# A fused decoder layer on one core: orders of their own for the first and last three turns, and the head weights turned in the double bank

## The reference

```python
x = layernorm(x + attn(x, W_attn, W_proj))           # 16 heads of 8, causal
x = layernorm(x + xattn(x, ctx, ctx, WQ, WK, WV, WO, bO))   # 16 heads of 64, softmax
x = layernorm(x + ffn(x, router_w, router_b, expert_w))     # 16 experts, top 6
```

## Time and profile before

| what | value |
|---|---|
| median of 3 runs | 1102.06 us (1099.71 to 1102.68) |
| the profiled execution | 1102.16 us |
| its span | 1100.3 us |
| mean granted TensorE clock | 0.985 of full |
| instructions | 44821 |
| busy share: DVE, ACT, POOL | 90%, 68%, 36% |
| DMA moved | 25.15 MB, mean 23 GB/s |

### The profile page before, as it was taken

One profiled execution on the slowest core, in us unless ns is written; L12 is line 12 of the kernel. 1 busy time (PEld: TensorE's weight loads), 2 busy tenths in 40 slices (PEclk: granted clock), 3 DMA queues, 4 the chain that ended last, 5 costly groups with the idle time before them and its releaser, 6 DMA issues.

```text
span 1100.3 us, 44821 instructions
## 1 busy us (share of the span) xinstructions
PE 1026.7 (93%) x16344; PEld 873.7 (79%) x16344; DVE 987.3 (90%) x3179; ACT 752.7 (68%) x1608; POOL 398.4 (36%) x682
## 2 busy tenths in 40 slices
PE   4789999999999999999999999999999999999874
PEld 3678888888888888888888888888888888888763
DVE  5579999999999999999999999999999999999776
ACT  4577876667787666777666678766677876667541
POOL 3232343433344333334433333434333443333331
PEclk8899999999999999999999999999999999999997
DMA  6000000000000000000000000000000000000000
GB/s 159 21 21 22 27 26 25 19 10 19 24 24 24 24 19 5 24 24 24 24 19 13 16 24 24 24 24 19 10 19 24 24 24 24 19 5 16 7 7 10
DMA packets 29577, 25.15 MB, mean 23 GB/s; under 512 B 2528, under 2 KB 24544, under 8 KB 29536
## 3 DMA queue, kind: packets, MB, share of 16 engines
q1 hardware_dynamic: 29536, 24.57, 7.7%
HBM read 20.37 MB, written 4.19 MB: 22 GB/s over the span
## 4 chain that ended last, share of the span: by engine, by line
PE 69%; DVE 14%; issue 6%; POOL 5%; ACT 4%; ACTq 0%; DMA 0%; DVEq 0%; POOLq 0%; SPq 0%
PE ps_B L349 54%; PE ps_S L349 10%; DVE sums L769 8%; PE ps_B L476 5%; POOL rstd L905 2%; DVE stats L692 2%; DVE ps_B L769 2%; ACT x L647 1%; ACT yT L545 1%; DVE p L748 1%; PE ps_B L435 1%; POOL shift L907 1%; POOL rstd L902 1%; DVE mv L698 1%; POOL minus_mean L903 1%
## 5 line engine op out<-in xcount | busy, mean ns | idle before, releaser
L769 DVE SCALAR_TENSOR_TENSOR sums<-ps_B,gate,sums 128x128 f32<-128x128 f32 x896 | 242.7, 345 | 9.9 <-PE ps_B L349 4.7
L902 POOL TENSOR_TENSOR rstd<-mv,ln_eps_tile 128x2 f32<-128x2 f32 x96 | 18.9, 197 | 522.9 <-DVE mv L698 522.9
L912 POOL TENSOR_TENSOR p<-p,rowinv 128x1024 f32<-128x1024 f32 x64 | 122.0, 1907 | 129.2 <-DVE rowinv L725 129.2
L545 ACT ACTIVATE q2T<-ps_B 128x512 f32<-128x512 f32 x128 | 73.2, 601 | 133.0 <-PE ps_B L349 133.0
L349 PE MATMUL ps_B<-wo_sb,oT 128*128 128x128 f32 x1024 | 122.8, 278 | 0.0
L647 ACT ACTIVATE x<-ps_B,shift,rstd 128x128 f32<-128x128 f32 x192 | 77.5, 456 | 63.1 <-POOL shift L907 62.7
L349 PE MATMUL ps_B<-ex_hi,x2T_hi 128*128 128x512 f32 x256 | 114.7, 448 | 5.5 <-POOL x2T_lo L886 4.3
L349 PEld LDWEIGHTS ps_B<-wo_sb,oT 128*128 128x128 f32 x1024 | 116.7, 192 | 2.2
L349 PE MATMUL ps_B<-ex_lo,x2T_hi 128*128 128x512 f32 x256 | 101.9, 398 | 0.0
L349 PE MATMUL ps_B<-ex_hi,x2T_lo 128*128 128x512 f32 x256 | 101.7, 397 | 0.0
L736 DVE SCALAR_TENSOR_TENSOR allowed<-ps_B,const 128x512 f32<-128x512 f32 x128 | 87.6, 684 | 9.2 <-ACT relu L567 8.9
(11 more groups left out here) (120 smaller groups left out, 2930.8 us busy)
## 6 DMA issues: line engine op xcount, KB each, us to landing
xT<-in_x_t SPq DMA_DIRECT2D x32, 256.0 KB, 2.7
...
```

The lines of the kernel that those rows point to most:

```text
L545: return nc.scalar.activation(dst, src, ACT.Copy, scale=scale)
L769: done = V.scalar_tensor_tensor(after, ps[BANK[f"FF{4 * r + q}"]][:, C * e:C * e + C], gate[:, r, 4 * q + e:4 * q + e + 1], before, ALU.mu ...
L912: G.tensor_tensor(weights, weights, rowinv[:, r].unsqueeze(2).broadcast_to([P, H, T]), ALU.mult).then_inc(p2_ready, 1)
```

## The change

Turns -2, -1 and 0 and turns 30, 31 and 32 get lists of their own for each engine, in which every step carries its turn (`K@-1`, `FF0@NT`), so a step of a later turn can stand before steps of an earlier one. Turns 1 to 29 keep the old lists. The counting of bank fills is adapted. The six heads jobs become three (one for queries, keys and values each, eight transposes) in the bank S, early in turns -2 and -1, each waiting for its own load; the copies and differences of them become 1024 wide. `experts_hi` goes from GpSimd to ScalarE, and the expert weights are loaded into the room of oT, so the first `AC0` copy waits for `experts_lo`. The first loads are put in another order, and VectorE splits W_attn before it makes the masks. A part of the diff:

```diff
+FIRST = {
+    "SP": """
+        x_columns@-2 x_rows@-1 context@-1 x_columns@-1 x_columns@0 x_rows@0 context@0
+    """,
+    "PE": """
+        Q@-2 K@-2 heads0@-2 V@-2 S1_0@-2 S1_1@-2 S1_2@-2 S1_3@-2 heads1@-2 K@-1 Q@-1 Y@-1 V@-1 heads2@-2 PR@-1 S1_0@-1
+        S1_1@-1 K2_3@-1 K2_0@-1 K2_2@-1 X1T@-1 S1_2@-1 S1_3@-1 Q2_3@-1 Q2_1@-1 Q2_0@-1 K2_1@-1 V2_3@0 K@0 Q2_2@-1 Y@0 S2_0@0
+        Q@0 PR@0 V@0 V2_0@0 V2_1@0 V2_2@0 S2_1@0 X1T@0 K2_0@0 Q2_3@0 PT0b@0 PT0a@0 S1_0@0 S1_1@0 K2_2@0 K2_3@0 AC0@0 K2_1@0
+        S1_2@0 PT1b@0 PT1a@0 S1_3@0 AC1@0 WO0@0 WO1@0 Q2_1@0 Q2_0@0 Q2_2@0 X2T@0 LG@0
+    """,
+    "ACT": """
+        K@-2 queries_hi@-2 heads_hi0@-2 relu0@-2 relu1@-2 square0@-2 square1@-2 V@-2 relu2@-2 relu3@-2 square2@-2
+        heads_hi1@-2 square3@-2 K@-1 experts_hi@-2 queries_hi@-1 Y@-1 V@-1 heads_hi2@-2 relu0@-1 relu1@-1 square0@-1 K2_0@-1
+        norm1@-1 K2_3@-1 K2_2@-1 square1@-1 x1_hi@-1 relu2@-1 relu3@-1 square2@-1 square3@-1 Q2_3@-1 Q2_1@-1 Q2_0@-1 K2_1@-1
...
+    "DVE": """
+        keys_lo0@-2 keys_lo1@-2 queries_lo@-2 heads_lo0@-2 allow0@-2 allow1@-2 pieces0@-2 pieces1@-2 p1_0@-2 allow2@-2
+        p1_1@-2 allow3@-2 pieces2@-2 pieces3@-2 p1_2@-2 p1_3@-2 keys_lo0@-1 heads_lo1@-2 keys_lo1@-1 queries_lo@-1
+        projected@-1 stats1@-1 var1@-1 allow0@-1 heads_lo2@-2 pieces0@-1 allow1@-1 p1_0@-1 pieces1@-1 x1_lo@-1 p1_1@-1
+        allow2@-1 allow3@-1 pieces2@-1 pieces3@-1 p1_2@-1 p1_3@-1 row_max0@0 projected@0 less_max0@0 stats1@0 var1@0
+        keys_lo0@0 keys_lo1@0 row_sum0@0 row_inv0@0 queries_lo@0 x1_lo@0 row_max1@0 less_max1@0 row_sum1@0 row_inv1@0
...
+    "POOL": """
+        next_x_hi@-2 context_hi@-1 next_x_lo@-2 context_lo@-1 root1@-1 experts_lo@-2 next_x_hi@-1 bias_x1@-1 next_x_lo@-1
+        root1@0 context_hi@0 context_lo@0 shares0@0 shares1@0 next_x_hi@0 root2@0 next_x_lo@0 x2_hi@0 bias_x1@0 x2_lo@0
+    """,
+}
+LAST = {
...
+    "PE": """
+        S2_0@NT-2 Y@NT-2 PR@NT-2 V2_3@NT-2 V2_0@NT-2 S2_1@NT-2 V2_1@NT-2 V2_2@NT-2 X1T@NT-2 FF0@NT-2 PT0a@NT-2 PT0b@NT-2
+        Q2_3@NT-2 K2_0@NT-2 K2_3@NT-2 K2_2@NT-2 K2_1@NT-2 AC0@NT-2 FF4@NT-2 PT1a@NT-2 PT1b@NT-2 FF5@NT-2 FF1@NT-2 AC1@NT-2
+        WO0@NT-2 WO1@NT-2 FF2@NT-2 FF6@NT-2 Q2_1@NT-2 FF7@NT-2 FF3@NT-2 X2T@NT-2 Q2_0@NT-2 Q2_2@NT-2 LG@NT-2 S2_0@NT-1
+        S2_1@NT-1 FF0@NT-1 V2_3@NT-1 V2_0@NT-1 V2_1@NT-1 PT0b@NT-1 V2_2@NT-1 FF4@NT-1 PT0a@NT-1 AC0@NT-1 FF5@NT-1 PT1a@NT-1
+        PT1b@NT-1 FF1@NT-1 AC1@NT-1 WO0@NT-1 WO1@NT-1 FF2@NT-1 FF6@NT-1 FF7@NT-1 FF3@NT-1 X2T@NT-1 LG@NT-1 FF0@NT FF4@NT
+        FF5@NT FF1@NT FF2@NT FF6@NT FF7@NT FF3@NT
+    """,
+    "ACT": """
...
+        norm2@NT-2 X2T@NT-2 Q2_0@NT-2 Q2_2@NT-2 logit_exp@NT-2 norm3@NT-2 exp0@NT-1 V2_3@NT-1 V2_0@NT-1 V2_1@NT-1 exp1@NT-1
+        PT0b@NT-1 V2_2@NT-1 PT0a@NT-1 base3@NT-1 AC0@NT-1 PT1a@NT-1 PT1b@NT-1 AC1@NT-1 norm2@NT-1 X2T@NT-1 logit_exp@NT-1
+        norm3@NT-1 base3@NT norm3@NT
+    """,
+    "DVE": """
...
+        gate1@NT-2 var3@NT-2 row_max0@NT-1 less_max0@NT-1 gate2@NT-1 gate3@NT-1 gate4@NT-1 gate5@NT-1 gate6@NT-1
+        row_sum0@NT-1 gate7@NT-1 row_inv0@NT-1 row_max1@NT-1 gate8@NT-1 less_max1@NT-1 gate9@NT-1 gate10@NT-1 gate11@NT-1
+        gate12@NT-1 row_sum1@NT-1 gate13@NT-1 row_inv1@NT-1 gate14@NT-1 gate15@NT-1 weigh0@NT-1 weigh1@NT-1 attended@NT-1
+        stats2@NT-1 var2@NT-1 weigh2@NT-1 weigh3@NT-1 logits@NT-1 gate0@NT-1 gate1@NT-1 stats3@NT-1 var3@NT-1 gate2@NT
...
+    "POOL": """
+        root1@NT-2 shares0@NT-2 context_hi@NT-2 context_lo@NT-2 shares1@NT-2 bias_x1@NT-2 root2@NT-2 root3@NT-2 x2_hi@NT-2
+        x2_lo@NT-2 shares0@NT-1 shares1@NT-1 root2@NT-1 x2_hi@NT-1 x2_lo@NT-1 root3@NT-1 root3@NT
+    """,
+}
...
+        def turns(eng, body, engine, order):
+
+            for word, turn in by_turn(FIRST[engine]):
+                body(turn, [word])
+            for i in range(1, 3):
+                body(i, order)
             with eng.Fori(3, NT - 3) as i:
...
+                body(i, order)
+            body(NT - 3, order)
+            for word, turn in by_turn(LAST[engine]):
+                body(turn, [word])
...
             load(xT, x_t, xT_in, 0)
+            sp.dma_start(w_attn_sb[:], w_attn).then_inc(attn_in, 16)
+            sp.dma_start(const[:], consts).then_inc(const_in, 16)
+            for dst, src, arrived in zip(heads_ld, (wq_t, wk_t, wv_t), heads_in):
+                sp.dma_start(dst, src).then_inc(arrived, 16)
+            load(cT, ctx_t, cT_in, 0)
+            load(x_sb, tile_x, x_in, 0)
+            sp.dma_start(ex_ld.rearrange("p (e n) -> p e n", e=E), expert_w.rearrange("e p n -> p e n")).then_inc(expert_in, 16)
...
+                def heads(what):
+
+                    pe.wait_ge(const_in, 16)
+                    pe.wait_ge(heads_in[what], 16)
+                    for j in range(J):
+                        last = pe.transpose(ps["S"][:, P * j:P * j + P], heads_ld[what][:, P * j:P * j + P], ident)
+                    return last
...
+                def experts_high():
+                    act.wait_ge(expert_in, 16)
+                    copy(ex_hi[:], ex_ld).then_inc(expert_hi, 1)
```

More of the change, by code:

```diff
@@ L90 @@
     p1_0 allow1 gate14 pieces1 gate15 p1_1 weigh0 allow2 weigh1 pieces2 allow3 p1_2 pieces3 attended stats2 var2
-    weigh2 p1_3 weigh3 logits stats3 gate0 var3 gate1 heads_lo0 heads_lo1 heads_lo2 heads_lo3 heads_lo4 heads_lo5
+    weigh2 p1_3 weigh3 logits stats3 gate0 var3 gate1
 """.split()
 POOL_ORDER = """
-    root1 shares0 context_hi context_lo shares1 root2 next_x_hi next_x_lo root3 bias_x1 x2_hi x2_lo experts_hi
-    experts_lo
+    root1 shares0 context_hi context_lo shares1 root2 next_x_hi next_x_lo root3 bias_x1 x2_hi x2_lo
@@ L104, in last_of, with by_turn @@
+def by_turn(words):
+    pairs = []
+    for word in words.split():
+        name, turn = word.split("@")
+        pairs.append((name, NT + int(turn[2:] or 0) if turn.startswith("NT") else int(turn)))
+    return pairs
+FIRST_JOBS, LAST_JOBS = by_turn(FIRST["PE"]), by_turn(LAST["PE"])
 def last_of(order, steps):
@@ L111, in stages, with fills, latest, place @@
     return ({"setup"} if turn == -2 else set()) | {s for s, t in (("s1", turn + 2), ("l1", turn + 1), ("l2", turn), ("ff", turn - 1)) if 0 <= t < NT}
[L114 to L127, removed]
+def fills(bank, jobs, before=None):
+    if before is not None:
+        jobs = jobs[:jobs.index(before)]
+    return sum(BANK[job if isinstance(job, str) else job[0]] == bank for job in jobs)
 ALL = {"s1", "l1", "l2", "ff"}
+STEADY_JOBS = [job for job, _, stage in JOBS if stage != "setup"]
+STAGE = {job: stage for job, _, stage in JOBS}
 def earlier(turn, job):
     bank = BANK[job]
[L137 to L140, removed]
+    if isinstance(turn, int) and turn <= 0:
+        return fills(bank, FIRST_JOBS, (job, turn))
+    first = fills(bank, FIRST_JOBS)
+    if isinstance(turn, int) and turn >= NT - 2:
+        return first + (NT - 3) * fills(bank, STEADY_JOBS) + fills(bank, LAST_JOBS, (job, turn))
+    return (turn - 1) * fills(bank, STEADY_JOBS) + (first + fills(bank, STEADY_JOBS, job))
+def latest(turn, jobs, waited=()):
+    def place(job):
+        if isinstance(turn, int) and turn <= 0:
+            return FIRST_JOBS.index((job, turn))
+        if isinstance(turn, int) and turn >= NT - 2:
+            return LAST_JOBS.index((job, turn))
+        return STEADY_JOBS.index(job)
+    return [job for job in jobs if BANK[job] not in waited and job == max((other for other in jobs if BANK[other] == BANK[job]), key=place)]
 def decoder(nc, x, x_t, ctx_t, w_attn, w_proj, wq_t, wk_t, wv_t, wo, b_o, router_t, router_b, expert_w, consts, out):
@@ L517, in body @@
                 numbered = {"heads": heads, "Q2_": q2, "K2_": k2, "V2_": v2_part, "S2_": s2, "AC": ac, "WO": wo_turn, "FF": ff}
-                for job, bank, stage in JOBS:
-                    if stage not in on(i):
+                for job in words:
+                    bank = BANK[job]
+                    if STAGE[job] not in on(i):
                         continue
```

137 lines of the change are left out of this document (67 added, 70 removed), and 4 rows, old and new, of the table JOBS.

## The result

The changed kernel took **1084.38 us** (median of 4 runs, 1083.51 to 1088.16), against 1102.37 (1099.71 to 1102.87) for the kernel before in the same set of runs: a ratio of 0.985, 95% interval 0.9838 to 0.9863. The forecast was 1087.2 with a range of 1081 to 1095. A repeat in another set of runs gave 1085.65 (1084.21 to 1088.25) and 0.9845 (0.9827 to 0.9863). The profiled execution took 1083.81, its span is 1082.0; that of the repeat 1086.01 and 1084.2.

The account below looks back on a forecast made before the run. TensorE, busy 93% of the span, was taken as the bound, with nearly all its idle time in head and tail. Head 9.2 plus tail 5.8 gave 15.0 us off 1102.16, so 1087.2 us, range 1081 to 1095.

Parts of the forecast that it names:

- One premise: Whole kernel: nearly all TensorE idle time is in head and tail, 26.7 and 23.0 us.
- Opening and ScalarE's queue: Head: 0.7 us gained before S1; ScalarE's queue delays yT, so tile 0's residual comes at 28.1 against 29.38.
- S1 and Q2 of tile 1: Head: passes run back to back without the relu hole; S2_0 of turn 0 at 42.0 against 49.68, 7.7 us.
- Rival (b), the clock: Head: TensorE's clock stays up with less idle time, worth 4.7 us more, about 1082 us; chance 0.15.
- Turn 0: From S2_0 of turn 0 to that of turn 1: 1.5 us gained, between 0 and 3.
- Turn 30: Tail, S2_0 of turn 30 to that of turn 31: 30.0 against 31.05 us, 1.1 gained.
- S2_1 ahead of V2_3, and exp1: Turn 31: S2_1 straight after less_max0, exp1 not behind V2 and PT0 copies; shares1 at 60.7 against 63.19.
- x2 ahead of root3: Tail: x2 pair before root3 removes FF's 4.35 us wait for tile 31; weigh0 at 80.6 against 86.45.
- geps "still runs beside shares1": Turn 31: geps still takes 1.74 us beside shares1, so base3 ends at 63.1.
- The tail's total: From S2_0 of turn 30 to the end: 5.8 us gained, bounds 2 and 8.
- Middle: From S2_0 of turn 1 to that of turn 30: unchanged, 938 to 940 us.
- rival (c), longer loop turns: Loop turns 1 to 29 get longer; at 0.7 us a turn the time is 1107 us; chance 0.07.

Follow-up runs that it names:

- first lists alone: Changed kernel with the new lists for the first three turns but the old order for the last three: 1091.72 us, ratio 0.9902.
- V2_3 ahead: Changed kernel with TensorE's V2_3 of turn 31 put back ahead of S2_1 of that turn: 1083.99 us, ratio 0.9829.
- FF0 later: Changed kernel with TensorE's FF0 of turn 31 moved behind the V2 jobs: 1085.85 us, ratio 0.9845.
- root3 first: Changed kernel with GpSimd's root3 of tile 30 put back ahead of x2_hi and x2_lo of tile 31: 1087.88 us, ratio 0.9869.
- the filler: Changed kernel plus 44 TensorE matmuls that nobody reads, also called the idle matmuls, ahead of K of tile 1: 1086.36 us, ratio 0.9855.
- experts_hi behind yT: Changed kernel with ScalarE's experts_hi moved behind queries_hi, Y and V of turn -1: 1087.5 us, ratio 0.9861.

## Why the prediction was right, and where it was off

The sign, the size and the split were as argued, and the experiments show the cause: with the same banks and first loads the new order of the first turns takes 9.4 us off the median, the last lists 6.8. One premise was read too strongly: head and tail held 49.7 us of TensorE's idle time, but the middle held 23.9, so two thirds and not nearly all. The change took 12.4 us of idle time from head and tail (26.7 to 19.2 and 23.0 to 18.1) and 1.7 from the middle. By steps:

**Opening and ScalarE's queue: right.** xT_hi at 18.95 (19.49 before), K of tile 1 at 20.96 (forecast 21.6), experts_hi 1.91 us (2.0), queries_lo ending 27.8 (28.0), residual 27.68 (28.1). ScalarE didn't wait for the expert weights. Y of tile 0 starts at 22.52, before 26 as asked.

**S1 and Q2 of tile 1: right in mechanism, 1.4 us too small.** S2_0 of turn 0 came at 40.58, not 42.0. I counted the passes end to end at 0.69 us each; back to back they overlap, two in 1.28 us (37.31), and passes with splits took 8.98 us where I had 10.0 to 10.4. That is the whole miss of the sum. The slow stretch at 33.6, which I meant to keep, has no term in it, and this execution didn't have one. The runs with the same head show the two cases: where the clock fell again ahead of S2_0 (granted 0.72 from 33 to 39 us with the first lists alone, 0.87 from 27 to 40 with V2_3 ahead), S2_0 of turn 0 is at 41.58 and 41.07; where it didn't, in the changed kernel, its repeat, FF0 later and root3 first, it is at 40.58, 39.33, 40.11 and 40.46. The landing of xT is in these too; from the residual to S2_0 it is 14.1 us in the first two and 12.8 to 12.9 in the others. VectorE's last pass starts 10.1 to 10.2 us behind the residual in all six, so the 1.2 us come behind the passes, where TensorE has Q2 and K2 left.

**Rival (b), the clock: true in its mechanism, its price not settled.** The clock does stay up with the shorter gaps in most executions, though my sum kept the slow stretches. A stretch at the lower level from 34.2 to 37.6 us costs 1.2 us; in the kernel before it was longer (32.8 to 39.6), and a second one (49.9 to 53.3) lay at the start of turn 0. No kernel here has the new lists with a slow stretch there, so how much of turn 0's gain is order and how much is clock isn't separated. The 3.5 us of busy time that TensorE saved in the head bound what the clock can have given as work; what of it lay on the chain is open. So part of the match is luck: the gain I credited to order alone is order plus a clock that rose because of the order. The Trainium skill, TensorE: Matmul & The Clock Gate, section HAM oscillation, says that idle gaps throttle the engine again; the traces agree, as the filler shows (0.62 to 1.00).

**Turn 0: 1.93 us for 1.5**, within its bounds, with the clock in it as said.

**Turn 30: 1.73 us for 1.1**; 29.3 us in every kernel with the last lists. TensorE was busy 27.41 us of it where I took the 27.91 of before.

**S2_1 ahead of V2_3, and exp1: wrong step.** The prediction said that S2_1 comes after less_max0 instead of after the bank, and that exp1 "no longer stands behind V2 and PT0 copies". It does stand behind three V2 copies in ScalarE's new list, and these waited for FF0 and V2_3 on a TensorE that had the lower level for a part of the time (1039.7 to 1043.1 us). With FF0 behind them exp1 is 0.7 us earlier; where the lower level lasted twice as long (the repeat, the idle matmuls, experts_hi behind yT) it is 1.1 to 1.3 later. From S2_0 of turn 31 to shares1 it took 12.68 us, against 13.06 before and 11.7 in my sum: 0.4 us gained, not 1.4. The table gives the stages of the tail in us, each from the one before it.

| kernel | turn 30 | S2_0 to exp1 | exp1 to shares1 | shares1 to weigh0 |
|---|---|---|---|---|
| before | 31.05 | 10.37 | 2.69 | 23.26 |
| changed | 29.32 | 10.01 | 2.67 | 19.66 |
| changed, repeat | 29.35 | 11.26 | 2.67 | 19.64 |
| first lists alone | 31.02 | 10.23 | 2.69 | 24.18 |
| root3 first | 29.32 | 10.08 | 2.67 | 22.15 |
| V2_3 ahead | 29.33 | 9.55 | 2.67 | 19.65 |
| FF0 later | 29.32 | 9.33 | 2.67 | 20.17 |

**x2 ahead of root3: right.** 3.6 us from shares1 to weigh0, where my numbers gave 23.26 - 19.9 = 3.4. Of it 2.5 is this order; which part of the other 1.1 is due to geps (0.10 us instead of 1.74) and which to the orders of TensorE and VectorE wasn't tried. The 24.18 of the first lists alone, with the old tail and a longer slow stretch, suggests that the clock alone can move this stage by 0.9. That geps "still runs beside shares1" was wrong by the list and not by chance: the old order has gate12 and gate13 between row_inv1 and geps (gate14), the new one of turn 31 has geps straight behind row_inv1, which also releases shares1. In all ten profiles with the new last lists geps begins 0.16 or 0.17 us before shares1 and takes 0.10 us; in the three with the old ones it begins 0.18 after and takes 1.73 or 1.74. The tail's total came out at 5.7 for 5.8 by luck (4.1 in the repeat's profile): turn 30 gave 0.6 more than forecast and the stretch to shares1 1.0 less.

**Middle.** From S2_0 of turn 2 to that of turn 30 it is 905.98 us before and 905.68 after; rival (c), longer loop turns, did not happen, nor in any other kernel (905.58 to 906.31). The 1.26 us of turn 1 (32.88 against 31.62) I take for an accident of the one profile of before, in which TensorE paused 1.31 us, see the last section; that profile has no second to hold it against.
